# Graph layer on one core: an order of the loop in which the small products, the last odd message, the permutations and the class sums stand elsewhere

## The chip, the core and the metric

The kernel runs on one core of one Trainium2 chip. The metric is the device time of one execution in microseconds (us), lower is better. Five engines run queues of their own, each strictly in the order of its program, and meet through semaphores: TensorE (PE; its weight loads are a row of their own, PEld), VectorE (DVE), ScalarE (ACT), GpSimd (POOL, here the issuer of the indirect DMAs) and SyncE (SP, issuer of plain loads).

## The reference

A message passing layer over a graph with 6250 nodes and 206250 edges, features of 64, hidden width 128, all in float32:

```python
msg = jnp.concatenate([src_node_features[col], edge_attr], axis=1)
h = jax.nn.relu(msg @ W1a.T + b1a)
h = h @ W1b.T + b1b
sums = jax.ops.segment_sum(h, row, num_segments=n_nodes)
agg = sums / jnp.maximum(counts, 1.0)[:, None]
z = jax.nn.relu(jnp.concatenate([src_node_features, agg], axis=1) @ W2a.T + b2a) @ W2b.T + b2b
out = jnp.concatenate([z, src_node_features], axis=1) @ Wr.T + br
return layernorm(x + out)
```

`col` is the sorted end of each edge, `row` (the one summed over) is not sorted. The edges are therefore sorted by `row` on the chip while the messages are computed.

## The kernel before

**Tiles.** The edges are cut into 403 quads of 512 edges. A turn `m` of the main loop (202 of them, behind 22 turns of preparation) starts quads `2m` and `2m+1`. Nodes are 49 classes of 128. Every 31 quads are a block (13 in all), for which the places in the sorted store are worked out.

**What a quad goes through.** PE `hidden(q)` (L561) is the first layer: one float32 product of 512 columns into the bank HH. ACT `relu(q)` (L837) moves it to `hT`. PE `message(q, j)` (L570), j from 0 to 3, is the second layer: a float32 product of 64 columns with 128 weights of `hT` into the one bank MS, which holds the eight results of a pair of quads. ACT `copy_x` (L850) takes the whole bank MS as bfloat16, DVE `rest` (L1039) the remainder, ACT `middle_part` (L856) and DVE `low` (L1045) the second and third parts. So each float32 number is three bfloat16 numbers in Z. PE `permute(q, h)` (L591), h 0 and 1, is 6 products of 195 columns into PA or PBk with the 0/1 matrices M that DVE `places(q, h)` (L1054) makes; ACT `evict(q, h)` (L888) brings the bank to `stg`, and POOL scatters it to the sorted store `region` (L1348).

**Ranks.** PE `rank(i)` has four small products: L629 (counts of quad i+42, bank CK), L684 and L689 (ranks of quad i+5, 200 columns each, bank RK) and L700 (destination steps of quad i+4, 6 columns, bank RK). DVE `ranks(i)` answers with `positions(i+5)` (L1059), every fourth time with `destinations` (L1114, L1118), and once in a block each with `chain_counts`, `chain_places` and `chain_steps`. At its place in `rank(i)` PE waits for the positions before. Once in a block DVE also has `index` (L1003 to L1012). DVE further makes `classes` (L1021), `onehot` (L1031) and `stair` (L1105).

**Sums.** From turn 145 on, 46 turns (`sum_at`) also gather one class of the first segment back from `region`: ACT `ids` (L867), DVE `same_node` (L1179), 30 PE products of 195 columns in `class_sum` (L604, into columns 200 and up of bank RK), DVE `add_class`. Three further classes, all of the second segment and the node layers follow behind the loop. Those gathers may start only when the last scatter has landed.

**Order within a turn before.** PE: `hidden(2m)`, both halves of `permute(2m-3)`, `hidden(2m+1)`, `message(2m, 0)`, `rank(2m)` (in sum turns with `class_sum` behind L629), `permute(2m-2)` with the messages 1 to 3 of quad 2m among its products, `rank(2m+1)` with the messages 0 to 3 of quad 2m+1 among its products. From turn 142 (EARLY) on message 0 of the even quad stands inside the permutation. DVE: `ranks(2m-1)`, `rest` twice, the first `places` with `low` twice between, `classes`, `onehot`, `ranks(2m)`, `add_class`, `stair`, `places` of the next quad, `same_node` of the next sum. ACT: `relu`, `middle_part` twice, `evict` twice, `relu`, `ids`, `evict` twice, `copy_x`.

Waits that matter: `message(q, 0)` of an even quad waits until DVE has done both `rest` of the pair before (L567, `s_r`), for they read MS. `rest` waits for `copy_x` (`s_x`), `copy_x` for the last message of the odd quad (`s_msg`).

## Time and profile before

| | us |
|---|---|
| median of 3 runs | 1556.19 |
| lowest and highest | 1556.15, 1567.82 |
| span of the profiled execution | 1549.2 |
| PE busy | 1504.9 (97%) |
| DVE busy | 1403.3 (91%) |
| POOL busy | 1066.0 (69%) |
| ACT busy | 1040.7 (67%) |

The profiled execution's span, from its first to its last instruction, lies 7.0 us under the median of the runs. How to read: "busy" is the time in which an engine has at least one instruction under way. The chain that ended last is for 83% of the span on PE. TensorE's granted clock is 0.992 of full speed (2.4 GHz) over the span, and 1.00 in all of the main loop.

### The profile page before, as it was taken

The page shows a single profiled execution, that of the slowest core. Times are in us where ns is not written, and L with a number is a line of the kernel's source. Part 1 is how long each engine was busy: PE and PEld are TensorE (multiplying, and loading weights), DVE is VectorE, ACT ScalarE, POOL GpSimd, SP SyncE. Part 2 cuts the span into 40 slices and gives each one's busy share as a digit, 9 for nine tenths or more (in the row PEclk, how much of TensorE's full clock was granted, in tenths as well). Part 3 has the DMA queues.
Part 4 walks back from the last instruction along what each step waited for, and adds up shares of the span by engine and source line. Part 5 has one row for each costly group of instructions (what it writes and reads, how often), then busy time and mean ns, then how long its engine had stood idle before and what let it go on. Part 6 is the DMA issues. An engine that isn't in the chain of part 4 may idle for free.

```text
span 1549.2 us, 42475 instructions
## 1 busy us (share of the span) xinstructions
PE 1504.9 (97%) x13326; PEld 1246.8 (80%) x13326; DVE 1403.3 (91%) x4381; ACT 1040.7 (67%) x2211; POOL 1066.0 (69%) x929
## 2 busy tenths in 40 slices
PE   9999999999999999999999999999999999996897
PEld 6788888888888888888888888888888888876776
DVE  5899999999999999999999999999999999886886
ACT  2687878778777887878877775656555665672222
POOL 2467777677776777767777777778777777766541
PEclk9999999999999999999999999999999999998999
DMA  8566656566666665656656669999999999785997
GB/s 231 154 172 171 167 161 179 165 167 177 164 174 169 166 178 161 169 164 177 166 161 180 174 202 290 275 292 301 290 283 294 268 301 289 222 260 198 368 365 236
DMA packets 135506, 336.23 MB, mean 217 GB/s; under 512 B 36506, under 2 KB 69565, under 8 KB 129016
## 3 DMA queue, kind: packets, MB, share of 16 engines
q0 software_dynamic: 53184, 225.39, 45.2%
q1 hardware_dynamic: 81028, 104.05, 26.4%
q10 hardware_dynamic: 1076, 4.09, 1.0%
q8 instruction: 112, 1.84, 0.5%
q14 instruction: 106, 0.87, 0.2%
HBM read 213.48 MB, written 119.91 MB: 215 GB/s over the span
## 4 chain that ended last, share of the span: by engine, by line
PE 83%; DMA 5%; DVE 5%; issue 2%; POOL 2%; ACT 1%; POOLq 0%; DVEq 0%; ACTq 0%; SPq 0%
PE HH L561 22%; PE MS L570 19%; PE PA L591 12%; PE PBk L591 12%; PE RK L604 7%; DMA gbuf<-region,idx 4%; PE RK L684 2%; PE CK L629 2%; PE RK L689 2%; PE PA L604 1%; DVE OH L1179 1%; POOL region L1348 1%; DMA region<-stg,dest 1%; DVE M L1054 1%; POOL gbuf L1376 1%
## 5 line engine op out<-in xcount | busy, mean ns | idle before, releaser
L1348 POOL DMA_INDIRECT region<-stg,dest x806 | 932.0, 1156 | 380.1 <-issue 190.9
L570 PEld LDWEIGHTS MS<-W,hT 128*128 128x128 f32 x3224 | 478.8, 191 | 68.0 <-issue 62.7
L570 PE MATMUL MS<-W,hT 128*128 128x64 f32 x3224 | 509.4, 260 | 0.0
L561 PE MATMUL HH<-eab,pw 128*128 128x512 f32 x806 | 433.7, 620 | 1.9 <-ACT hT L837 1.9
L1054 DVE TENSOR_SCALAR M<-pos_of,pos 128x384 bf16<-128x384 int16 x1612 | 431.3, 318 | 0.2
L591 PE MATMUL PBk<-Z,M 128*128 128x195 bf16 x2418 | 338.7, 248 | 0.2 <-ACT stg L888 0.2
L591 PE MATMUL PA<-Z,M 128*128 128x195 bf16 x2418 | 315.2, 248 | 7.8 <-ACT stg L888 6.5
L888 ACT ACTIVATE stg<-PA 120x585 bf16<-120x585 f32 x403 | 263.5, 654 | 88.0 <-PE PA L591 82.2
L591 PEld LDWEIGHTS PA<-Z,M 128*128 128x128 bf16 x2418 | 214.0, 103 | 125.5 <-issue 119.9
L837 ACT ACTIVATE hT<-HH 128x512 f32<-128x512 f32 x403 | 241.9, 600 | 84.2 <-PE HH L561 84.2
L888 ACT ACTIVATE stg<-PBk 120x585 bf16<-120x585 f32 x403 | 265.3, 658 | 47.2 <-PE PBk L591 45.7
L591 PEld LDWEIGHTS PBk<-Z,M 128*128 128x128 bf16 x2418 | 233.8, 107 | 0.6 <-issue 0.4
L1059 DVE TENSOR_REDUCE pos<-RK 128x4 f32<-128x200 f32 x403 | 146.7, 364 | 49.0 <-PE RK L700 34.2
L856 ACT ACTIVATE Z<-Zr 128x256 bf16<-128x256 f32 x403 | 146.9, 413 | 52.7 <-DVE Zr L1039 52.4
L850 ACT ACTIVATE Z<-MS 128x512 bf16<-128x512 f32 x202 | 122.2, 605 | 85.4 <-PE MS L570 85.4
L1045 DVE TENSOR_TENSOR Z<-Zr,Z 128x256 bf16<-128x256 f32 x403 | 169.8, 421 | 4.6
L1179 DVE TENSOR_TENSOR OH<-laneb,ids 128x1920 bf16<-128x1920 bf16 (+2 forms) x110 | 161.8, 1487 | 12.5 <-ACT ids L867 12.4
L1039 DVE TENSOR_TENSOR Zr<-MS,Z 128x256 f32<-128x256 f32 x403 | 151.1, 415 | 16.4 <-ACT Z L850 16.2
L1031 DVE TENSOR_SCALAR eab<-kb,C 64x1024 f32<-64x1024 bf16 x202 | 153.1, 758 | 7.5 <-DMA kb<-keyd 1.0
L604 PEld LDWEIGHTS RK<-gbuf,OH 128*128 128x128 bf16 x1440 | 122.8, 97 | 22.4 <-issue 17.3
L604 PE MATMUL RK<-gbuf,OH 128*128 128x195 bf16 x1440 | 130.5, 247 | 3.1 <-DVE OH L1179 1.5
L561 PEld LDWEIGHTS HH<-eab,pw 128*128 128x128 f32 x806 | 122.0, 192 | 3.9 <-issue 3.7
(214 smaller groups left out, 1524.3 us busy)
## 6 DMA issues: line engine op xcount, KB each, us to landing
eab<-in_ea SPq DMA_DIRECT2D x201, 256.0 KB
kb<-keyd SPq DMA_DIRECT2D x201, 128.0 KB
pw<-ptab SPq DMA_DIRECT2D x403, 32.0 KB
region<-stg,dest POOLq DMA_INDIRECT x806
gbuf<-in_xt ACTq DMA_DIRECT2D x6, 422.5 KB
ptab<-OH SPq DMA_DIRECT2D x7, 256.0 KB, 3.2
gbuf<-region,idx POOLq DMA_INDIRECT x98, 8.9
eab<-in_xt SPq DMA_DIRECT2D x12, 130.0 KB
```

The costliest lines, as they stand in the source:

```text
L561: e.matmul(HH[:, :], pw[:, q % 4, :], eab[:, c % NB, at_q:at_q + GE], start=True, stop=True).then_inc(s_h, 1)
L570: ins = e.matmul(MS[:, o:o + D], hT[:, q % 2, 128 * j:128 * j + 128], W[:, W_1B:W_1B + D], start=True, stop=True)
L591: last = e.matmul(P[:, 256 * j:256 * j + 3 * PART].rearrange("p (k f) -> p k f", k=3), M[:, q % 2, 2 * h + t, j, :], Z[:, q // 2 % 2, 4 * ...
L604: last = e.matmul(o, onehots(s, c)[:, k, j, :], rows[:, ROW * k + LINE * j:ROW * k + LINE * j + 3 * PART], start=k == 0 and j == 0, stop=k ...
L837: e.activation(hT[:, q % 2, :], HH[:, :], ACT.Relu).then_inc(s_relu, 1)
L888: e.activation(stb[:, g % NS, :].rearrange("p (j f) -> p j f", j=R)[:, :, 0:3 * PART], P[0:KC, 0:768].rearrange("p (j f) -> p j f", j=R)[: ...
L1031: e.tensor_scalar(eab[64:128, c % NB, 0:w], kb[64:128, c % NB, 0:w], C[64:128, C_P64:C_P64 + 1], None, ALU.is_equal).then_inc(s_oh, 1)
L1039: e.tensor_tensor(Zr[:, j:j + 4, :], MS[:, j * D:j * D + 4 * D].rearrange("p (j f) -> p j f", f=D), Z[:, q // 2 % 2, j:j + 4, 0, 0:D], ALU ...
L1045: e.tensor_tensor(Z[:, q // 2 % 2, j:j + 4, 2, 0:D], Zr[:, j:j + 4, :], Z[:, q // 2 % 2, j:j + 4, 1, 0:D], ALU.subtract).then_inc(s_l, 1)
L1054: last = e.tensor_scalar(M[:, q % 2, t, :, :], pos_of[:, :, :], pos[:, q % 16, t:t + 1], None, ALU.is_equal)
L1179: last = e.tensor_tensor(onehots(s, c).rearrange("p k j (n u) -> p (k j) n u", u=2)[:, k:k + n, :, :], lane2[:, None, :, :].to_broadcast([ ...
L1348: e.indirect_dma_start(lines[s], bass.IndirectOffsetOnAxis(ap=dest[:, g:g + 1], axis=0), stw[:, g % NS, :], None).then_inc(s_sc[g % NS], 16)
```

## The change

- `rank`: L700 with its wait moves from behind L689 to ahead of L684. The wait for the positions is a function `bank_read` now. Message 3 of the odd quad leaves `rank` and is issued in the next turn, right behind `hidden` of the even quad.
- Permutations come half a turn later: `permute(2m-4)` behind that message, `permute(2m-3)` in the second half of the turn, with messages 1 to 3 of the even quad.
- `rank(2m)` stands before `hidden(2m+1)`, and `message(2m, 0)` always directly behind `hidden(2m+1)` (EARLY is gone). `class_sum` comes behind that message.
- A semaphore `s_even` tells `relu` of an even quad that its half of `hT` is free.
- ACT and DVE lists follow: `copy_x` comes behind the first `relu`; on DVE `same_node` (in a sum turn) or `places(2m-3)` and `classes` (in another) stand ahead of `rest`.

```diff
@@ schedule of the gathers
-        gather_at = {2 * (m - 3) - 2: c for m, c in sum_at.items()}
-        gather_at.update({2 * (max(sum_at) + k): NC - BEHIND + k for k in range(BEHIND)})
+        gather_at = {max(2 * (m - 3) - 3, BQ * SEGB[1] + NS // 2 - 1): c for m, c in sum_at.items()}
+        gather_at.update({2 * (max(sum_at) + k) - 1: NC - BEHIND + k for k in range(BEHIND)})
@@ PE, message
+                        if j == 3 and q % 2 == 0 and q < NQ - 1:
+                            ins.then_inc(s_even, 1)
@@ PE, rank
+                        bank_read(i)
...
-                        if i % 2 == 0 and i // 2 in sum_at:
-                            class_sum(sum_at[i // 2])
...
+                        q = i + 4
+                        if 0 <= q < NQ:
+                            b = q // BQ
+                            e.wait_ge(s_S, q // 2 + 1)
+                            k = 4 * (q % BQ)
+                            at_q = Q_DEST + 6 * (q % 4)
+                            last = e.matmul(RK[:, at_q:at_q + 6].rearrange("p (k g) -> p k g", g=2), S[:, q % 4, :],
+                                            Dzb[:, b % 2, :, k + 1:k + 4:2], start=True, stop=True)
                         q = i + 5
...
-                        if beside is not None:
-                            message(beside, 3)
-                        q = i + 4
-                        if 0 <= q < NQ:
...
@@ PE, a turn
                             hidden(2 * f)
-                        if 0 <= 2 * m - 3 < NQ:
-                            permute(2 * m - 3, 0)
-                            permute(2 * m - 3, 1)
+                        if m - 1 in front and 2 * front[m - 1] + 1 < NQ:
+                            message(2 * front[m - 1] + 1, 3)
+                        if 0 <= 2 * m - 4 < NQ:
+                            permute(2 * m - 4, 0)
+                            permute(2 * m - 4, 1)
+                        if m < 0:
+                            spin(e, HH, 4)
+                        rank(2 * m)
                         even = odd = None
...
                             hidden(odd)
-                        if even is not None and m < EARLY:
+                        if even is not None:
                             message(even, 0)
-                        if m < 0:
-                            spin(e, HH, 4)
-                        rank(2 * m)
-                        if 0 <= 2 * m - 2 < NQ:
-                            permute(2 * m - 2, 0, even)
-                            permute(2 * m - 2, 1, even)
+                        if m in sum_at:
+                            bank_read(2 * m + 1)
+                            class_sum(sum_at[m])
+                        if 0 <= 2 * m - 3 < NQ:
+                            permute(2 * m - 3, 0, even)
+                            permute(2 * m - 3, 1, even)
@@ ACT, relu
-                            e.wait_ge(s_msg, q // 2)
+                            e.wait_ge((s_even, s_msg)[q % 2], q // 2)
@@ ACT, a turn (the new order)
                             relu(2 * f)
                         if m - 1 in front:
+                            copy_x(front[m - 1])
+                        if 2 * m - 1 >= AMID[PB - 1]:
+                            copy_chain(2 * m - 1)
+                        if 0 <= 2 * m - 4 < NQ:
+                            evict(2 * m - 4, 0)
+                            evict(2 * m - 4, 1)
+                        copy_chain(2 * m)
+                        if f is not None and 2 * f + 1 < NQ:
+                            relu(2 * f + 1)
+                        if m - 1 in front:
                             for q in range(2 * front[m - 1], 2 * front[m - 1] + of_pair(front[m - 1])):
                                 middle_part(q)
...
+                        if next_sum(m) is not None:
+                            ids(0, next_sum(m))
                         if 0 <= 2 * m - 3 < NQ:
                             evict(2 * m - 3, 0)
                             evict(2 * m - 3, 1)
@@ DVE, a turn (the new order)
                         ranks(2 * m - 1)
+                        if m in sum_at:
+                            same_node(0, sum_at[m])
+                        elif 0 <= 2 * m - 3 < NQ:
+                            places(2 * m - 3, 0)
+                            places(2 * m - 3, 1)
+                        if 0 <= m + LEAD // 2 < NP and m not in sum_at:
+                            classes(m + LEAD // 2)
                         f = front.get(m - 1)
                         if f is not None:
                             for q in range(2 * f, 2 * f + of_pair(f)):
                                 rest(q)
...
+                        ranks(2 * m)
+                        if 0 <= m + LEAD // 2 < NP and m in sum_at:
                             classes(m + LEAD // 2)
                         if m + 1 in front:
                             onehot(front[m + 1])
-                        ranks(2 * m)
+                        if m in sum_at and 0 <= 2 * m - 3 < NQ:
+                            places(2 * m - 3, 0)
+                            places(2 * m - 3, 1)
+                        if f is not None:
+                            for q in range(2 * f, 2 * f + of_pair(f)):
+                                low(q)
                         if m in sum_at:
                             add_class(sum_at[m])
                         if 0 <= m + 3 < NP:
                             stair(m + 3)
-                        if 0 <= 2 * m - 1 < NQ:
-                            places(2 * m - 1, 0)
-                            places(2 * m - 1, 1)
+                        if 0 <= 2 * m - 2 < NQ:
+                            places(2 * m - 2, 0)
+                            places(2 * m - 2, 1)
```

## Rows read from the trace of the kernel before

**Rows 1.** The page: the span, and busy time (share of span) xinstructions.
```profile
span 1549.2 us, 42475 instructions
...
PE 1504.9 (97%) x13326; PEld 1246.8 (80%) x13326; DVE 1403.3 (91%) x4381; ACT 1040.7 (67%) x2211; POOL 1066.0 (69%) x929
```
**Rows 2.** Timeline of a plain turn: start us, us, engine line op tiles [idle before].
```profile
605.27 0.25 PE L689 MATMUL RK<-BS,sel 128*128 128x200 bf16 x1
...
605.36 0.36 PE L570 MATMUL MS<-W,hT 128*128 128x64 f32 x2
...
605.58 1.10 PE L561 MATMUL HH<-eab,pw 128*128 128x512 f32 x2
605.76 0.60 ACT L850 ACTIVATE Z<-MS 128x512 bf16<-128x512 f32 x1 [0.37 <-PE MS L570]
605.79 0.36 DVE L1059 TENSOR_REDUCE pos<-RK 128x4 f32<-128x200 f32 x1
...
606.07 0.17 DVE L1114 TENSOR_REDUCE dsum<-RK 120x8 f32<-120x24 f32 x1
...
606.42 0.75 DVE L1039 TENSOR_TENSOR Zr<-MS,Z 128x256 f32<-128x256 f32 x2
606.52 0.68 PE L591 MATMUL PA<-Z,M 128*128 128x195 bf16 x6
...
607.22 0.71 ACT L856 ACTIVATE Z<-Zr 128x256 bf16<-128x256 f32 x2
...
607.56 1.05 PE L561 MATMUL HH<-eab,pw 128*128 128x512 f32 x2
...
608.44 0.33 PE L570 MATMUL MS<-W,hT 128*128 128x64 f32 x2
...
608.47 0.42 DVE L1045 TENSOR_TENSOR Z<-Zr,Z 128x256 bf16<-128x256 f32 x1
...
608.61 0.25 PE L629 MATMUL CK<-OC,ind 128*128 128x200 bf16 x1
...
608.80 0.38 DVE L1021 TENSOR_TENSOR OC<-clsb,cls 128x400 bf16<-128x400 bf16 x1
...
608.89 0.51 PE L591 MATMUL PA<-Z,M 128*128 128x195 bf16 x4
...
610.39 0.31 DVE L1105 TENSOR_TENSOR S<-iotab,offs 128x240 bf16<-128x240 bf16 x1
...
610.50 0.36 PE L570 MATMUL MS<-W,hT 128*128 128x64 f32 x2
...
610.62 1.04 DVE L1054 TENSOR_SCALAR M<-pos_of,pos 128x384 bf16<-128x384 int16 x4
...
611.56 1.10 PE L561 MATMUL HH<-eab,pw 128*128 128x512 f32 x2
```
**Rows 3.** Timeline of a sum turn, the same columns.
```profile
1157.54 2.15 DVE L1179 TENSOR_TENSOR OH<-laneb,ids 128x3840 bf16<-128x3840 bf16 x1
...
1158.06 1.10 PE L561 MATMUL HH<-eab,pw 128*128 128x512 f32 x2
...
1159.61 0.36 DVE L1059 TENSOR_REDUCE pos<-RK 128x4 f32<-128x200 f32 x1
...
1166.62 1.10 PE L561 MATMUL HH<-eab,pw 128*128 128x512 f32 x2
```
**Rows 4.** Timeline of DVE where a block's work comes in, two stretches.
```profile
475.63 0.27 DVE L1003 TENSOR_TENSOR kd<-dc,baseB 128x124 int32<-128x124 int32 x1
...
476.62 0.35 DVE L1059 TENSOR_REDUCE pos<-RK 128x4 f32<-128x200 f32 x1
...
488.96 0.21 DVE L1072 CAST offs<-RK 128x62 bf16<-128x62 f32 x1
...
489.92 0.74 DVE L1039 TENSOR_TENSOR Zr<-MS,Z 128x256 f32<-128x256 f32 x2
```
**Rows 5.** Timeline of POOL at the end of the loop.
```profile
1401.10 0.99 POOL L1348 DMA_INDIRECT region<-stg,dest  x1 [0.30 <-issue]
```

More of the change, by code:

```diff
@@ L61 @@
 PIECES = 5
-EARLY = SUMS - 3
 SUMCOL = 200
@@ L596, in permute @@
                                     last.then_inc((s_pA, s_pB)[h], 1)
-                                if beside is not None and (h, j, t) in among(beside):
-                                    message(beside, among(beside)[h, j, t])
+                                if beside is not None and (h, j, t) in among:
+                                    message(beside, among[h, j, t])
                     def products(o, s, c):
@@ L612, in class_sum, with bank_read @@
                         products(sums(c), 0, c)
-                    def rank(i, beside=None):
-                        if not pe_ranks(i):
-                            for j in range(4 if beside is not None else 0):
-                                message(beside, j)
-                            return
-                        if beside is not None:
-                            message(beside, 0)
-                        last = None
-                        b = block_at(i - 1, 12)
-                        if b is not None:
-                            e.wait_ge(s_cc, COPIES * b + 2)
-                        q = i + 42
-                        if 0 <= q < NQ:
-                            e.wait_ge(s_oc, q // 2 + 1)
-                            k = q % BQ
-                            last = e.matmul(CK[:, 0:4 * CL], ind[:, 30 - k:158 - k],
-                                            OC[:, q % OCN, :, :].rearrange("p t c -> p (t c)"),
-                                            start=k == 0, stop=k == BQ - 1)
-                        if beside is not None:
-                            message(beside, 1)
+                    def bank_read(i):
                         if 0 <= i + 4 < NQ:
@@ L651, in rank @@
                             e.wait_ge(s_tab[1], 12)
+                    def rank(i, beside=None):
+                        if not pe_ranks(i):
+                            for j in range(3 if beside is not None else 0):
+                                message(beside, j)
+                            return
+                        if beside is not None:
+                            message(beside, 0)
+                        last = None
+                        b = block_at(i - 1, 12)
+                        if b is not None:
+                            e.wait_ge(s_cc, COPIES * b + 2)
+                        q = i + 42
+                        if 0 <= q < NQ:
+                            e.wait_ge(s_oc, q // 2 + 1)
+                            k = q % BQ
+                            last = e.matmul(CK[:, 0:4 * CL], ind[:, 30 - k:158 - k],
+                                            OC[:, q % OCN, :, :].rearrange("p t c -> p (t c)"),
+                                            start=k == 0, stop=k == BQ - 1)
+                        if beside is not None:
+                            message(beside, 1)
+                        bank_read(i)
                         if i % 2 and i // 2 in sum_at:
                             e.wait_ge(s_ad, 3 * sum_at[i // 2] + 3)
-                        if i % 2 == 0 and i // 2 in sum_at:
-                            class_sum(sum_at[i // 2])
                         b = block_at(i, 11)
@@ L910, in _ @@
                             evict(2 * m - 3, 1)
-                        if f is not None and 2 * f + 1 < NQ:
-                            relu(2 * f + 1)
-                        copy_chain(2 * m)
                         if f is not None:
                             copy_id(f)
-                        if next_sum(m) is not None:
-                            ids(0, next_sum(m))
-                        if 0 <= 2 * m - 2 < NQ:
-                            evict(2 * m - 2, 0)
-                            evict(2 * m - 2, 1)
-                        if f is not None:
-                            copy_x(f)
                     for c in range(NC - BEHIND + 2, NC):
@@ L1233, in _ @@
                                 rest(q)
-                        if 0 <= 2 * m - 2 < NQ:
-                            places(2 * m - 2, 0)
-                        if f is not None:
-                            low(2 * f)
-                        if 0 <= 2 * m - 2 < NQ:
-                            places(2 * m - 2, 1)
-                        if f is not None and of_pair(f) == 2:
-                            low(2 * f + 1)
-                        if 0 <= m + LEAD // 2 < NP:
+                        ranks(2 * m)
+                        if 0 <= m + LEAD // 2 < NP and m in sum_at:
                             classes(m + LEAD // 2)
@@ L1262, in _ @@
                                 totals(s)
-                        if next_sum(m) is not None and m < NP - 2:
-                            same_node(0, next_sum(m))
                     def add(p):
```

25 lines of the change are left out of this document (7 added, 18 removed).

## The prediction

> **What bounds the kernel now.** I read the page first: PE is busy 97% of the span, DVE 91% [rows 1]. Then the timeline of a plain turn. `hidden` of the even quad starts at 605.58 and that of the next pair at 611.56: 5.98 us a turn, in which PE's products follow each other without a hole [rows 2]. A sum turn lasts from 1158.06 to 1166.62, 8.56 us [rows 3], just as dense. So time can be won only by a shorter stream of PE, and lost by anything that makes PE wait. What the reader has to see next is how much room each wait has. Take the start of `hidden` of the even quad as 0. DVE begins `positions` at 0.21 (605.79) and ends both `rest` at 1.59 (606.42 and 0.75), while the next message into MS stands at 2.86 (608.44) [rows 2]. That is over a microsecond of room before PE would wait for `rest`.
>
> **PE's stream after the change.** Now message 3, L700 and `hidden` take 1.16 together (605.36 to 606.52) [rows 2]. Afterwards `hidden` follows a 200-column product, as the odd one now follows one of 195: 0.88 (607.56 to 608.44). Message 3 follows `hidden`, as message 0 does now: 0.17 (608.44 to 608.61). L700 stands between two bfloat16 products: four of them take 0.28 (608.61 to 608.89), three of 200 columns at 0.085 each, so 0.03 for it. The sum is 1.08, which saves 0.08 a turn [rows 2]. It is float32 weights that lie open behind a short product and are covered behind a long one. In a sum turn message 0 too goes from among the permutations (three of them with 12 products take 1.61, 608.89 to 610.50, so 0.19 each) to behind `hidden`, 0.17: 0.11 in all. Of 202 turns 46 are sum turns (49 classes less 3), which leaves about 155 steps: 155 x 0.083 = **-13 us**, and a sum turn of 8.45 us if nothing waits.
>
> The Trainium skill (TensorE: Matmul & The Clock Gate, "Step-by-step: what each phase is for") says that the next tile's weights load while the present product runs. Taken plainly, the order of products would then cost nothing and the -13 would be 0. The row speaks against it here: the same `hidden` takes 0.94 behind the 6 columns of L700 and 0.88 behind 195 [rows 2].
>
> **The new place of `rest`.** The new PE times of a turn, from the same rows: `hidden` to 0.88, message 3 to 1.05, 12 permutation products of 1.04 (606.52 to 607.56) to 2.09, `rank` 0.28 to 2.37, `hidden` to 3.25, and there stands `message(2m, 0)`, which waits for both `rest`. ACT needs `relu` first: `middle_part` starts 0.70 after the end of `hidden` now (606.52 to 607.22), and `copy_x` takes that place: it starts at 1.58, ends at 2.18 (0.60), and `rest` can start 0.05 later, at 2.21 to 2.24 (now 606.36 to 606.42) [rows 2]. From the end of `rest` to the message I take 0.05 for the signal and 0.09 to 0.11 for the weights, an estimate from 1246.8 us for 13326 loads [rows 1]. So `rest` must end by **3.10**, or PE stands still. Behind that message on PE are the sums, the permutation, the second `rank` and the next `hidden`, so every engine waits with it.
>
> *Plain turn.* `rest` at its earliest ends at 2.21 + 0.75 = 2.97. DVE's list before it: `positions` 0.28 (605.79 to 606.07), every other turn `destinations` 0.35 (606.07 to 606.42), four `places` 0.96 (1.04 less an overlap of 0.08), `classes` 0.38 [rows 2]. DVE's start x follows from the turn before. `low` waits for `middle_part`, which waits for the odd `hidden`: 3.25 + 0.70 + 0.41 = 4.36, `low` at 4.39; then two `low` of 0.33 (608.47 to 608.80), `stair` 0.23 (610.39 to 610.62), `places` 0.96: 6.24, less the turn of 5.90 gives x = 0.35 [rows 2]. So `rest` ends at 0.35 + 0.28 + 0.35 + 0.96 + 0.38 + 0.75 = 3.07 in the longer case: just in time. I take 0 for the stall; the seams between DVE's instructions that are new here have no row, and by the neighbouring ones are off by up to 0.1, in one turn of two. Kept for the range: 0 to +0.05 a turn, +8 us.
>
> *Sum turn.* Here x is 0.21, since DVE waits for the rank product. Ahead of `rest` stand `positions` 0.28 and `same_node`, 2.07 (1157.54 to 1159.61) [rows 3]. `rest` ends at 0.21 + 0.28 + 2.07 + 0.75 = 3.31, with `destinations` at 3.66. That is 0.21 and 0.56 past 3.10, 0.39 on the mean. `class_sum` then waits for the positions made after `rest`, about 0.05 more (estimate). PE's turn is 8.45 + 0.44 = 8.89 against 8.56 now: +0.33, times 46 = **+15 us**. With seams of 0.1 either way: +10 to +20. Now nothing of that shows, as `same_node` straddles the turn's start and message 0 stands behind the sum.
>
> *Blocks.* A block brings DVE extra work: `index` 0.99 (475.63 to 476.62) and `chain_places` 0.96 (488.96 to 489.92) [rows 4], and `chain_counts`, `chain_runs` and `chain_steps`, three or so small operations each, which I put at 0.5 to 0.8 by the same rows. Now a microsecond of room takes them in. Afterwards what comes ahead of `rest` finds 0 to 0.3 us of room (3.10 less 2.97 to 3.07, and DVE's pause for `copy_x`). `index` at a turn's end costs about 0.5 to 0.7 us in the next turn; what falls into `ranks` of an odd index costs 0.4 to 0.7, `chain_places` in every other block, counts and steps in the others. What falls behind `rest` is mostly taken in by the pause before `low` (about 0.3). I take 1.2 us a block less 0.3 for waits of `rank` on positions and chain that go away, since `rank(2m)` and `rank(2m+1)` now lie more evenly: 12 blocks x 0.9 = **+11 us**, bounds 0 and 20.
>
> *End of the loop.* The last scatters go out back to back, one in 1.30 (0.99 and 0.30 idle) [rows 5], and the second segment's gathers wait for them. With the permutations half a turn later POOL has one quad, two scatters, more to do: **+2.6 us**, bounds 0 and 3.
>
> The other moves cost nothing: both `relu`, `evict` and the two halves of a permutation keep half a microsecond or more between producer and consumer by the times above. The gathers are issued one quad earlier in number, which is the same moment.
>
> **Sum.** -13 + 15 + 11 + 2.6 = +16 us on the span of 1549.2 [rows 1], so 1565 there. The span lies 7.0 under the median, and the edits are within it: 1556.2 + 16 = **1572 us**, 1.0% slower.
>
> **Rivals.**
> - *The stream alone decides (other side).* If the Vector chain of a sum turn ends by 3.10, because `same_node` and its seams are shorter by 0.2 to 0.5, and blocks are taken in, then 1556.2 - 13 - 46 x 0.11 + 2.6 = 1541. For it: PE is the one full engine. Against it: 2.07 for `same_node` is a plain row.
> - *Sums wait, blocks don't.* 1572 - 11 = 1561. For it: DVE has pauses in each turn, and blocks are 3 of 15 turns.
> - *DVE bounds the plain turns too.* x creeps past 0.4 and every second message waits 0.1: 1572 + 8 = 1580.
> - *The new order saves nothing on PE.* Then 1572 + 13 + 5 = 1590. The page's rule above would have it so; the row is against it.
> - *Gain and loss cancel*: the waits cost half of what I take, 1556.
>
> **How the numbers follow.** Forecast 0.42, stream alone 0.08, sums only 0.25, DVE everywhere 0.15, cancel 0.07, no saving 0.03. The range of 1554 to 1588 leaves out the stream alone and no saving, and about 0.08 of the others' edges. A measurement of this kernel can tell about 1%, 15.6 us, from no change, so the borders are 1540.6 and 1571.8. The forecast lies on the upper one and goes two to one to "slower", the sums-only and cancel cases to "same": faster 0.06, same 0.45, slower 0.49.
>
> **What would show it.** Right: plain turns of 5.89 to 5.90 between the even `hidden`; in sum turns of about 8.7 and 9.05 by turns, a pause of TensorE in front of L570 ended by DVE Zr L1039; in blocks the same pause, up to 0.7. Wrong: sum turns of 8.45 (no stall), plain turns of 5.98 (no gain of the stream) or over 5.95 (DVE bounds), a last scatter that isn't later against the last `hidden`.

## The result and the profile after

On the chip of the result the changed kernel takes 1580.76 us (median of 4 runs, 1578.32 to 1582.63), the kernel before 1561.8 beside it (4 runs, 1556.15 to 1567.82): ratio on record 1.0142, 95% interval 1.0107 to 1.0177. So it is slower, by 1.4% by that ratio and by 1.2% (19.0 us) by the medians alone; the ratios on record, here and below, are not the quotients of the two medians, and lie up to 0.7 points off them. The profiled spans are 1577.3 and 1549.2 [rows 1], 28.1 apart, 9 more than the medians. About 5 of these come from the profiles: that of before lies 7.0 under the median of its first runs, that of after 1.9 under its own run (1579.23).

The page of the changed kernel: span, busy time (share) xinstructions, then the chain that ended last by engine, and one of its costliest groups (busy, mean ns | idle before, releaser).

```profile
span 1577.3 us, 42707 instructions
PE 1507.1 (96%) x13326; PEld 1249.6 (79%) x13326; DVE 1391.7 (88%) x4381; ACT 1018.8 (65%) x2211; POOL 1064.0 (67%) x929
...
PE 77%; DVE 10%; DMA 4%; issue 4%; ACT 2%; POOL 2%; DVEq 0%; POOLq 0%; ACTq 0%
...
L570 PEld LDWEIGHTS MS<-W,hT 128*128 128x128 f32 x3224 | 501.5, 191 | 241.0 <-DVE Zr L1042 132.8
```

No engine has a larger share of the span than before [rows 1]; DVE's share of the chain has gone from 5% to 10%. A group of the page of before was "PEld MS L570 <- DVE Zr L1039", 4.9 us in 17 waits. The same waits after (us in total, times, longest):

```profile
PEld MS L570 <- DVE Zr L1042: 132.8, 188, 2.3
PE MS L570 <- DVE Zr L1042: 23.2, 43, 1.5
```

(`rest` is L1042 now, `positions` L1062, the destination product L687, the ranks L692 and L697, `permute` L590, `class_sum` L603, `same_node` L1182, `copy_x` L853, `evict` L891, the scatter L1354.)

**A plain turn.** Timeline, start us, us, engine, line. Where a list ends with a first layer "x1", it shows the first of its two passes alone, and the turn ends at its start:

```profile
606.90 0.25 PE L697 MATMUL RK<-BS,sel 128*128 128x200 bf16 x1
606.99 1.05 PE L561 MATMUL HH<-eab,pw 128*128 128x512 f32 x2
607.43 0.35 DVE L1062 TENSOR_REDUCE pos<-RK 128x4 f32<-128x200 f32 x1
607.87 0.33 PE L570 MATMUL MS<-W,hT 128*128 128x64 f32 x2
...
608.56 0.60 ACT L853 ACTIVATE Z<-MS 128x512 bf16<-128x512 f32 x1
...
609.16 0.17 PE L687 MATMUL RK<-Dz,S 128*128 128x6 bf16 x1
609.18 0.25 PE L692 MATMUL RK<-OC,trib 128*128 128x200 bf16 x1
...
609.25 0.75 DVE L1042 TENSOR_TENSOR Zr<-MS,Z 128x256 f32<-128x256 f32 x2
...
610.24 0.33 PE L570 MATMUL MS<-W,hT 128*128 128x64 f32 x2
...
612.88 0.62 PE L561 MATMUL HH<-eab,pw 128*128 128x512 f32 x1
```

From 606.99 to 612.88: 5.89 us, against 5.98 [rows 2]. `positions` starts 0.44 into the turn, `rest` ends at 3.01, the message that needs it stands at 3.25.

**A sum turn** (1242.76 to 1251.42, 8.66 us, against 8.56 [rows 3]):

```profile
1242.76 1.05 PE L561 MATMUL HH<-eab,pw 128*128 128x512 f32 x2
...
1243.24 2.15 DVE L1182 TENSOR_TENSOR OH<-laneb,ids 128x3840 bf16<-128x3840 bf16 x1
...
1245.12 1.05 PE L561 MATMUL HH<-eab,pw 128*128 128x512 f32 x2
1245.31 0.75 DVE L1042 TENSOR_TENSOR Zr<-MS,Z 128x256 f32<-128x256 f32 x2
...
1246.11 0.30 PEld L570 LDWEIGHTS MS<-W,hT 128*128 128x128 f32 x2 [0.77 <-DVE Zr L1042]
...
1246.39 2.73 PE L603 MATMUL RK<-gbuf,OH 128*128 128x195 bf16 x30
...
1251.42 0.62 PE L561 MATMUL HH<-eab,pw 128*128 128x512 f32 x1
```

`rest` ends 3.30 into the turn and TensorE's weight load for the message waits for it. In the next sum turn `destinations` are in front too: `rest` ends at 3.67, and the turn takes 9.04.

**A block.** `index` at the end of DVE's list, and the two turns behind it (95.92 to 102.69, 102.69 to 110.12):

```profile
96.38 0.27 DVE L1006 TENSOR_TENSOR kd<-dc,baseB 128x124 int32<-128x124 int32 x1
...
97.49 0.36 DVE L1062 TENSOR_REDUCE pos<-RK 128x4 f32<-128x200 f32 x1
...
99.15 0.74 DVE L1042 TENSOR_TENSOR Zr<-MS,Z 128x256 f32<-128x256 f32 x2
...
99.95 0.43 PE L570 MATMUL MS<-W,hT 128*128 128x64 f32 x2 [0.61 <-DVE Zr L1042]
...
105.42 0.26 PE L648 MATMUL CK<-OC,ind 128*128 128x200 bf16 x1 [0.48 <-ACT BS L879]
```

`positions` starts 1.57 into the turn instead of 0.44, `rest` ends at 3.97. One turn later `rank` waits for a copy of the block's chain.

**The first sum turn**, around turn 145, which starts at 931.97:

```profile
926.18 1.06 POOL L1373 DMA_INDIRECT gbuf<-region,idx  x1 [0.30 <-issue]
...
931.97 1.05 PE L561 MATMUL HH<-eab,pw 128*128 128x512 f32 x2
...
936.74 0.26 ACT L870 ACTIVATE ids<-gbuf 128x60 bf16<-128x60 bf16 x1 [6.00 <-DMA gbuf<-region,idx]
937.69 0.69 PE L590 MATMUL PA<-Z,M 128*128 128x195 bf16 x6 [4.50 <-ACT stg L891]
```

The first gather is issued 5.79 us ahead of its turn. Before it was 9.29 ahead (920.65 against 929.94). From issue to the start of `ids` it takes 10.56 us (926.18 to 936.74), before 10.46 (920.65 to 931.11), so the late issue comes out in full: ACT waits 6.00 for it, before 3.11. `evict` stands behind `ids` on ACT, and PE waits 4.50 for `evict`, before 1.01. Behind that pause the clock adds to it: from 938.2 to 941.6 TensorE's granted clock is 0.50 of full speed, its lower level (1.2 GHz), where it was 1.00 ahead of the pause and is again behind 941.6. Half of these 3.4 us, 1.7, is lost work. The turn takes 14.76; 8.45 without a wait, 4.50 and 1.7 make 14.65. Before, the turn took 10.27 and the clock stayed at 1.00.

**The ledger.** The starts of the even first layers cut both profiled spans into turns; after less before, in us:

| stretch | forecast | measured |
|---|---|---|
| turns 3 to 144, stream alone (142 x -0.088) | -13 (155 turns) | -12.5 |
| the same turns, excess of the nine blocks (+14.1) and of turns 123 and 124 | +11 (12 blocks) | +14.8 |
| turn 145, the first sum turn | none | +4.5 |
| turns 146 to 192 (32 undisturbed sum turns among them, 8.84 against 8.53 on the mean, +10.0) | +15 (46 turns) | +16.4 |
| turns 193 to 200 | none | +1.2 |
| behind the last first layer | +2.6 | +4.0 |
| ahead of turn 3 | none | -0.3 |
| sum | +16 | +28.1 |

In the row of turns 193 to 200, turn 197 alone is 1.67 longer: a pause of 2.74 in front of a permutation, before 2.24, and behind it the granted clock at 0.50 from 1399.0 to 1405.8.

### The profile page after: what moved, and what is told of

Read it like the earlier page. It is cut to its first block, busy times and chain, and to the rows that moved or that the text cites. A ratio compares the mean times of both kernels' runs of the same rounds, so it can differ in the third digit from the quotient of the medians.

```text
span 1577.3 us, 42707 instructions
## 1 busy us (share of the span) xinstructions
PE 1507.1 (96%) x13326; PEld 1249.6 (79%) x13326; DVE 1391.7 (88%) x4381; ACT 1018.8 (65%) x2211; POOL 1064.0 (67%) x929
## 4 chain that ended last, share of the span: by engine, by line
PE 77%; DVE 10%; DMA 4%; issue 4%; ACT 2%; POOL 2%; DVEq 0%; POOLq 0%; ACTq 0%
PE MS L570 18%; PE HH L561 18%; PE PBk L590 11%; PE PA L590 11%; PE RK L603 7%; DMA gbuf<-region,idx 3%; PE RK L692 2%; DVE M L1057 2%; DVE Zr L1042 2%; PE CK L648 2%; PE PA L603 2%; PE RK L697 2%; DVE OH L1182 1%; DMA region<-stg,dest 1%; POOL region L1354 1%
## 5 line engine op out<-in xcount | busy, mean ns | idle before, releaser
L1354 POOL DMA_INDIRECT region<-stg,dest x806 | 920.8, 1142 | 408.9 <-ACT stg L891 228.0
L570 PEld LDWEIGHTS MS<-W,hT 128*128 128x128 f32 x3224 | 501.5, 191 | 241.0 <-DVE Zr L1042 132.8
L570 PE MATMUL MS<-W,hT 128*128 128x64 f32 x3224 | 530.4, 260 | 23.6 <-DVE Zr L1042 23.2
L561 PE MATMUL HH<-eab,pw 128*128 128x512 f32 x806 | 424.1, 608 | 1.3 <-ACT hT L840 0.8
L840 ACT ACTIVATE hT<-HH 128x512 f32<-128x512 f32 x403 | 240.6, 597 | 261.0 <-PE HH L561 259.5
L891 ACT ACTIVATE stg<-PA 120x585 bf16<-120x585 f32 x403 | 265.6, 659 | 117.7 <-PE PA L590 114.2
L590 PE MATMUL PBk<-Z,M 128*128 128x195 bf16 x2418 | 339.2, 249 | 0.2 <-DVE M L1057 0.2
L590 PE MATMUL PA<-Z,M 128*128 128x195 bf16 x2418 | 306.1, 249 | 8.0 <-ACT stg L891 7.5
L891 ACT ACTIVATE stg<-PBk 120x585 bf16<-120x585 f32 x403 | 270.3, 671 | 20.4 <-PE PBk L590 17.2
L590 PEld LDWEIGHTS PA<-Z,M 128*128 128x128 bf16 x2418 | 228.9, 111 | 8.8 <-issue 7.9
L590 PEld LDWEIGHTS PBk<-Z,M 128*128 128x128 bf16 x2418 | 235.0, 108 | 0.8 <-DVE M L1057 0.4
L1048 DVE TENSOR_TENSOR Z<-Zr,Z 128x256 bf16<-128x256 f32 x403 | 153.6, 424 | 46.5 <-ACT Z L859 44.9
L1062 DVE TENSOR_REDUCE pos<-RK 128x4 f32<-128x200 f32 x403 | 143.3, 356 | 43.8 <-PE RK L697 40.8
L1182 DVE TENSOR_TENSOR OH<-laneb,ids 128x1920 bf16<-128x1920 bf16 (+2 forms) x110 | 161.7, 1486 | 17.4 <-ACT ids L870 17.1
L1042 DVE TENSOR_TENSOR Zr<-MS,Z 128x256 f32<-128x256 f32 x403 | 150.9, 415 | 13.2 <-ACT Z L853 11.7
L859 ACT ACTIVATE Z<-Zr 128x256 bf16<-128x256 f32 x403 | 144.6, 410 | 1.3 <-DVE Zr L1042 1.2
L603 PE MATMUL RK<-gbuf,OH 128*128 128x195 bf16 x1440 | 130.9, 247 | 2.4 <-DVE OH L1182 1.7
L561 PEld LDWEIGHTS HH<-eab,pw 128*128 128x128 f32 x806 | 121.7, 191 | 2.2 <-issue 1.9
L603 PEld LDWEIGHTS RK<-gbuf,OH 128*128 128x128 bf16 x1440 | 120.3, 97 | 2.8 <-issue 2.8
L853 ACT ACTIVATE Z<-MS 128x512 bf16<-128x512 f32 x202 | 121.3, 600 | 0.0
```

Source lines behind the costliest of these rows:

```text
L561: e.matmul(HH[:, :], pw[:, q % 4, :], eab[:, c % NB, at_q:at_q + GE], start=True, stop=True).then_inc(s_h, 1)
L570: ins = e.matmul(MS[:, o:o + D], hT[:, q % 2, 128 * j:128 * j + 128], W[:, W_1B:W_1B + D], start=True, stop=True)
L590: last = e.matmul(P[:, 256 * j:256 * j + 3 * PART].rearrange("p (k f) -> p k f", k=3), M[:, q % 2, 2 * h + t, j, :], Z[:, q // 2 % 2, 4 * ...
L603: last = e.matmul(o, onehots(s, c)[:, k, j, :], rows[:, ROW * k + LINE * j:ROW * k + LINE * j + 3 * PART], start=k == 0 and j == 0, stop=k ...
L840: e.activation(hT[:, q % 2, :], HH[:, :], ACT.Relu).then_inc(s_relu, 1)
L891: e.activation(stb[:, g % NS, :].rearrange("p (j f) -> p j f", j=R)[:, :, 0:3 * PART], P[0:KC, 0:768].rearrange("p (j f) -> p j f", j=R)[: ...
```

## The experiments

The runs of this section come from three different chips; whether the chip of the result is one of them isn't known. On them the kernel before took 1860.44, 1832.42 and 1862.82 us, 17 to 19% more than beside the result. So times are compared on one chip only, and mechanisms by turns that came through undisturbed. On none of the three was a profile of the kernel before taken; where turns are compared with it, the kernel before with L700 moved stands in for it.

**First chip: the destination product alone, in the kernel before.**

```diff
@@ rank, of the kernel before
+                        (L700 and its wait, ahead of L684)
                         q = i + 5
...
-                        (L700 and its wait, behind L689 and message 3)
```

> The kernel before, with one part of the change alone: L700 (destination product) and its wait stand ahead of L684 in rank. Nothing else moves. If the order of PE's stream is what gains (0.94 against 0.88 for a first layer behind 6 columns or behind 195): a plain turn of 5.92 instead of 5.98 and a sum turn of 8.50 instead of 8.56, no new wait, about 12 us faster than the kernel before, 1544 to 1549. If weight loads are hidden whatever the order: plain turns stay at 5.98 and the time stays at that of the kernel before.

Measured: 1867.02 (1850.92 to 1887.78, 10 runs) against 1860.44 (13 runs), ratio 1.0043 (0.9996 to 1.0091). The time is the same within the noise. Undisturbed turns took 5.946 (12 of them), against 5.977 on the chip of the result. The same kernel on the second chip:

> The kernel before with L700 ahead of L684 alone. In the first trace of it the undisturbed turns took 5.95 (not 5.92: I had left out that L700 costs 0.03 at its new place too). So 0.03 a turn, 6 us, faster than the kernel before where the stream of PE bounds (0.996), and no difference where DMAs bound.

Measured: 1836.66 against 1832.42, ratio 1.0015 (0.9981 to 1.0049); undisturbed turns again 5.946. So in the order of before the place of L700 is worth 0.03 us a turn, half of what I expected (the 0.03 that L700 takes at its new place I had left out), and no time that can be measured. In that order a first layer behind a message starts the next product 0.91 after itself (764.30 to 765.21, rows below), between the 0.94 behind L700 and the 0.88 behind 195 columns [rows 2].

**First chip: message 0 behind the class sum in sum turns, in the changed kernel.**

```diff
+                    def among(q):
+                        if q // 2 in sum_at:
+                            return {(0, 0, 1): 0, (0, 2, 0): 1, (1, 0, 1): 2, (1, 2, 0): 3}
+                        return {(0, 1, 1): 1, (1, 0, 1): 2, (1, 2, 0): 3}
...
-                        if even is not None:
+                        if even is not None and m not in sum_at:
                             message(even, 0)
```

> The changed kernel, but in sum turns message 0 of the even quad goes back among the permutation's products, behind the class sum. If two waits stand behind each other at that place (message 0 for rest, then the class sum for the positions that DVE makes after rest), taking the first away moves the stall to L603 and sum turns stay at about 8.65 and 9.0. If rest alone was the cause, sum turns fall to about 8.47 and the run is about 18 us faster than the changed kernel.

Measured: 1820.11 (one run). Undisturbed sum turns are not shorter: 8.86 and 8.81 where the changed kernel has 8.67 and 8.61. TensorE's pause now stands in front of `class_sum`: it starts 1.26 and 1.35 behind the odd first layer, where 0.88 would do, so the pause is 0.4 to 0.5 us, and 0.85 in the sum turns with `destinations` (9.19). In the undisturbed turns without `destinations` `class_sum` starts at 3.63 in both kernels. Two waits stood one behind the other: `class_sum` needs `positions`, which DVE makes behind `rest`. Taking the first away lays the second bare.

**Both waits taken away:** message 0 as above, and in sum turns DVE's `ranks(2m)` ahead of `rest`.

```diff
                         f = front.get(m - 1)
+                        if m in sum_at:
+                            ranks(2 * m)
                         if f is not None:
                             for q in range(2 * f, 2 * f + of_pair(f)):
                                 rest(q)
-                        ranks(2 * m)
+                        if m not in sum_at:
+                            ranks(2 * m)
```

> As the run before it, and in sum turns DVE answers rank(2m) (positions) ahead of both rest. Both waits are then off the path: sum turns of 8.45 to 8.50, 0.4 less than in the changed kernel, 46 of them, so 16 to 19 us faster than the changed kernel: 1562 to 1565. If something else holds the sum turns (gathers, the one-hots of same_node), they stay above 8.6.

Timeline of an undisturbed sum turn of this kernel (1532.25 to 1540.57; `class_sum` is L606 here, `rest` L1045, `same_node` L1185):

```profile
1532.25 1.05 PE L561 MATMUL HH<-eab,pw 128*128 128x512 f32 x2
...
1532.73 2.15 DVE L1185 TENSOR_TENSOR OH<-laneb,ids 128x3840 bf16<-128x3840 bf16 x1
...
1534.80 0.36 DVE L1065 TENSOR_REDUCE pos<-RK 128x4 f32<-128x200 f32 x1
1535.07 0.75 DVE L1045 TENSOR_TENSOR Zr<-MS,Z 128x256 f32<-128x256 f32 x2
1535.41 2.72 PE L606 MATMUL RK<-gbuf,OH 128*128 128x195 bf16 x30
...
1540.57 0.62 PE L561 MATMUL HH<-eab,pw 128*128 128x512 f32 x1
```

The sum starts 0.88 behind the odd first layer (1534.53) without a pause; the turn takes 8.33, where the changed kernel has 8.61 with the same work, and the other kind of turn 8.47 against 8.67. So in sum turns without `destinations` the stall is gone, and that shows its cause. With `destinations` ahead of both, a part of it stays: the least disturbed turns of that kind (168, 184 and 192) take 8.75, 8.72 and 8.49, where the changed kernel has 9.02, 8.96 and 8.96, and `class_sum` starts at 3.51, 3.54 and 3.32 instead of 3.25, 3.16 and 3.16. Against the one-wait kernel turns 146 to 192 are 13.9 us shorter in sum. Time: 1807.92 (1801.81 to 1814.26, 4 runs), ratio to before 0.9716 (0.9648 to 0.9784).

**The first sum turn: sums one turn later.**

```diff
-SUMS = 145
+SUMS = 146
```

> The changed kernel with all class sums one turn later (SUMS 146 instead of 145). Theory: the 14.8 us turn in which the sums begin comes from ScalarE, which waits for the first gather ahead of the evictions; the gather is issued half a turn later than before, as it hangs on a scatter of a permutation. One more turn of distance takes most of the 4.5 us of PE's pause away: 3 to 5 us faster than the changed kernel, the first sum turn below 11. Rival: the first gather takes as long as the DMA queues need to drain whenever it is issued; then the pause stays at 4 to 5 us.

Measured: 1813.99 (one run). Turns 144 to 146 take 9.11, 7.74 and 11.10, in sum 27.95; in the kernel with message 0 moved, on the same chip, they take 11.16, 10.14 and 9.24, 30.54. The 2.6 less is what a plain turn in place of a sum turn gives anyway, and that sum has to be done later; the first sum turn, 11.10, is not below the 11 that I expected either. But the run can't test the theory, for what was to be removed isn't there on this chip: in neither of the two kernels does ACT pause in front of the first `ids` (it starts 12.7 and 8.9 us behind the gather's issue; the result has a pause of 6.00 there). The gather did get more distance: it follows quad 283 instead of 282 (`gather_at`), while its sum went back by two quads. That a late gather is the cause of the long turn is therefore read from the rows of the result, where gather, `ids`, `evict` and permutation follow each other; it is not shown by an experiment.

**Second chip: the changed kernel.**

> The changed kernel once more, as the control for the others of this call. In the call before, the kernel before took 1860 us where the shown runs took 1556, with waits for landing DMAs throughout, so a chip is to be compared with itself alone. If the chip is as in the shown runs: 1.4% slower than the kernel before, plain turns 5.89, sum turns 8.67 and 9.04. If it is as in the call before: the order with the permutations half a turn later gives evictions and scatters more distance and the changed kernel is 2 to 3% faster than the kernel before, as the other variants of it were.

Measured: 1771.76 (1766.4 to 1780.99, 4 runs) against 1832.42 (13 runs): ratio 0.9635 (0.9588 to 0.9681). Here the changed kernel is *faster*, by 3.7% by that ratio and by 3.3% by the medians. By turns, against the kernel before with L700 moved: turns 3 to 144 -72.8 us, sum turns +10.3, behind the loop +9.2. The changed kernel loses in sum turns and at the end here too, but not in turn 145 (10.23 against 10.14); the gain ahead of it is another than in the result. The waits of both (us in total, times, longest), first the kernel before with L700 moved:

```profile
DVE pos L1059 <- remote: 184.7, 67, 4.3
...
ACT Z L850 <- remote: 100.2, 51, 3.0
PE HH L561 <- ACT hT L837: 98.5, 70, 2.6
```

and the changed kernel on the same chip:

```profile
PEld MS L570 <- DVE Zr L1042: 179.2, 165, 2.4
...
DVE pos L1062 <- remote: 104.5, 59, 5.6
...
ACT Z L853 <- remote: 5.9, 6, 1.1
...
PE HH L561 <- ACT hT L840: 2.4, 4, 1.2
```

"remote" is a releaser that the profile can't name. In the profiles of the chip of the result it does not occur among the larger waits, for either kernel. What it looks like (the kernel before with L700 moved, second chip):

```profile
764.02 0.25 PE L697 MATMUL RK<-BS,sel 128*128 128x200 bf16 x1
764.10 0.36 PE L570 MATMUL MS<-W,hT 128*128 128x64 f32 x2
764.30 1.08 PE L561 MATMUL HH<-eab,pw 128*128 128x512 f32 x2
765.21 0.68 PE L591 MATMUL PA<-Z,M 128*128 128x195 bf16 x6
...
767.64 0.37 DVE L1059 TENSOR_REDUCE pos<-RK 128x4 f32<-128x200 f32 x1 [4.12 <-remote]
767.68 0.60 ACT L850 ACTIVATE Z<-MS 128x512 bf16<-128x512 f32 x1 [2.92 <-remote]
...
768.18 0.59 ACT L837 ACTIVATE hT<-HH 128x512 f32<-128x512 f32 x1
...
768.91 1.47 PE L561 MATMUL HH<-eab,pw 128*128 128x512 f32 x2 [2.51 <-ACT hT L837]
```

L697 is over at 764.27 by its row, and `positions`, which reads its result, starts at 767.64; TensorE's semaphore events of all these products stand between 767.6 and 767.85 in the records. In the order of before, by the rows, ACT meets such a late signal in `copy_x` (L850), `relu` (L837) of the even quad stands behind it on ACT, and the odd first layer waits for `relu`: TensorE's gaps between a permutation and that first layer come to 120 us in turns 3 to 144 (84 gaps), those in front of the permutations behind `rank` to 48 (54). In the changed order `relu` of the even quad stands ahead of `copy_x`, and a whole permutation lies between message 3 and its reader. Both kinds of gap are gone (the wait of L561 for L840 is 2.4 us in the whole kernel); the largest kind now is the one between a first layer and the message behind it, 62 us (110 gaps). That the new lists of ACT and PE are the cause is read from the waits; no run changes them alone.

The 72.8 us of turns 3 to 144 split into TensorE's idle time, 160.0 against 111.3 (49 less), and its busy time, 943.25 against 919.08 (24 less). Of the 24 the stream gives 8 (142 x 0.057). The other 16 fit the granted clock, which differs a good deal: in these turns it is at the lower level for 109 us in the order of before (26 stretches) and for 31 us in the changed one (7 stretches), 0.95 and 0.99 on the mean, with 1.00 for both kernels beside the result. So part of the gain is most likely a clock that falls less often; it can't be split from the waits here, since the falls may themselves come of the pauses.

> The changed kernel with message 0 behind the class sum and the positions ahead of rest in sum turns. Expected from the undisturbed sum turns of its first trace: 8.47 where DVE has no destinations to make and 8.74 where it has, mean 8.60, against 8.67 and 9.04, mean 8.86. 46 turns: 10 to 13 us faster than the changed kernel, about the time of the kernel before plus 10 on a chip as in the shown runs.

Measured: 1763.6 (1752.85 to 1787.42, 4 runs), ratio to before 0.9558 (0.9505 to 0.961). Turns 146 to 192 are 13.1 us shorter than in the changed kernel on the same chip, at the upper end of what I expected. The median is 8 us lower, and the ranges of the runs overlap; without the one run of 1787.42 the other three have a median of 1758.77, 13 lower.

> As the run before it, and with two more moves: the sums begin one turn later (SUMS 146), and DVE's index of a block stands behind onehot, in DVE's pause ahead of low, instead of at the turn's end. Theory of the blocks: index at the turn's end pushes rest past 3.10 and costs 0.87 or 1.16 a block (turns of 6.77 and 7.05 instead of 5.89); in the pause it costs 0.3 or less: 12 blocks, 7 to 10 us. First sum turn: 3 to 5 us. Together 10 to 15 us faster than the run before it, which on a chip as in the shown runs is at the time of the kernel before or a few us under it. Rival: index delays low, stair and places of its turn by the same amount and PE then waits for those.

Its edit beside the two above is SUMS 146 and `index` moved up:

```diff
                         if m + 1 in front:
                             onehot(front[m + 1])
+                        for i in (2 * m + LEAD + 2, 2 * m + LEAD + 3):
+                            if i % BQ == 0 and 0 < i < NQ:
+                                index(i // BQ)
```

Measured: 1758.75 (1744.13 to 1770.47, 4 runs), ratio 0.9548 (0.9469 to 0.9628), the lowest median on this chip. I had expected 10 to 15 us less than the run before it; it is 4.9, with ranges that overlap, so a gain of the two added moves is not shown.

**Third chip.** The changed kernel as the base:

> The changed kernel once more, beside the kernel before on whatever chip this lands on, as the base for the next three. Theory 1 (the verdict belongs to the chip: where the kernel before takes about 1556 us the change costs some 1.4%, where it takes 1830 us or more the change gains some 3.5%): 1.010 to 1.018 in the first case, 0.96 to 0.97 in the second. Theory 2 (the 0.9635 was of one chip alone and the slow chips differ among each other): a ratio between 0.98 and 1.00 on a slow chip.

Measured: 1809.16 (1794.97 to 1814.92, 4 runs) against 1862.82 (7 runs), ratio 0.9697 (0.9627 to 0.9766). Theory 1 holds as far as it was tried: where the kernel before takes 1556 us the change loses, and where it takes 1830 or more it gains 3 to 4%, twice. Whether it is the chip or the hour that makes the difference, these runs don't tell apart.

> The changed kernel with message 0 behind the class sum and ranks(2m) ahead of rest in sum turns, index behind onehot instead of at the turn's end, and SUMS 146. If the waits of the first layer's neighbours on rest are what the changed kernel loses: sum turns of 8.33 and 8.47 undisturbed (46 x 0.33 = 15 us less), turn 145 of 7.7 and a first sum turn of 11.1, index turns 0.5 to 0.8 shorter than in the changed kernel; 18 to 25 us less than the changed kernel in the same call, and faster than the kernel before on a fast chip too (about 1558 against 1562, ratio 0.995 to 1.000; on a slow chip 0.95 to 0.96). If the waits only move (rival): within 5 us of the changed kernel.

Measured: 1792.94 (1789.38 to 1797.53, 4 runs), ratio 0.962 (0.9566 to 0.9673), 16 us below the changed kernel, where I expected 18 to 25. Turns 146 to 192 are 7.8 shorter than there, turns 3 to 144 6.3 longer, which is noise of that chip as far as I can tell. So this version is ahead of both kernels on two chips; under the conditions of the result it wasn't tried.

> The changed kernel with index moved from the turn's end to behind onehot, in the same turn, all else as it is. If index costs what was forecast (0.5 to 0.7 in the next turn, for rest comes later by it): turns behind an index lose their pause in front of the message, in all 12 times 0.5 to 0.9, 6 to 10 us. If the pause in those turns comes from something else of the block (chain_runs at the same place): the same turns stay as long as in the changed kernel.

Measured: 1809.89 (one run), no gain. The nine stretches of three turns around an `index` (up to turn 144) have medians of 23.2 us, and 22.9 in the changed kernel on the same chip. But this chip can't show what was asked. In its plain turns far from a block `positions` starts 1.82 into the turn in the median, in the changed kernel 1.75, where the result has 0.45; in the turn behind an `index` it starts between 0.24 and 3.60, in the changed kernel between 0.25 and 1.98. The 1.1 us by which an `index` delays it in the result is lost in that. So the expected gain of 6 to 10 us did not show in one run, and whether the place of `index` in DVE's list matters stays open. In the profile of the result DVE pauses in a plain turn 0.36 ahead of `low` (605.48, ended by ACT L859) and, in turns without `destinations`, 0.44 ahead of `rest` (603.31, ended by ACT L853), so there is little room for 1.0 us of extra work at either place.

> The changed kernel with the destination product back behind the two rank products, where the kernel before has it (6 columns directly ahead of message 0 to 2 or of the next first layer). If a first layer behind 6 columns lies open by its weights and behind 200 columns doesn't: undisturbed plain turns of 5.95 to 5.97 instead of 5.89, and the first layer of the even quad 0.06 longer. If the place is free (rival): 5.89 to 5.90.

```profile
481.81 0.17 PE L698 MATMUL RK<-Dz,S 128*128 128x6 bf16 x1
481.84 1.10 PE L561 MATMUL HH<-eab,pw 128*128 128x512 f32 x2
482.78 0.33 PE L570 MATMUL MS<-W,hT 128*128 128x64 f32 x2
```

Measured: 1803.41 (one run; the total says nothing on 10 us here). The six undisturbed plain turns take 6.015 in the median, against 5.889: +0.126, twice what I expected. The first layer behind the 6 columns takes 0.94 (481.84 to 482.78), behind 200 columns 0.88 (606.99 to 607.87), and this happens twice a turn, since `rank(2m)` now stands ahead of the odd first layer too. This shows the stream's gain to be the place of the destination product: without it, the new order would have been slower than before in plain turns as well (6.015 against 5.977). Within the first layer the rows put the 0.06 between its two passes: the second starts 0.51 behind the first when 6 columns stand ahead (605.58 to 606.10 before), 0.45 when 195 do (607.56 to 608.01), with weight loads of 0.19 in both. That fits weights that lie open, but what the run shows is the place alone.

## Why the prediction was right, and where it was off

- *Plain turns.* Forecast 5.89 to 5.90, measured 5.89. The removal shows that the gain is the product ahead of the first layer; that it is the weights which lie open behind 6 columns fits the rows. The reading of "message 3, L700 and `hidden`" as one sum of 1.16 hid that the move pays twice in the new order and that the rest of the order costs 0.04.
- *Sum turns.* Forecast 8.7 and 9.05 by turns, measured 8.67 and 9.04; `rest` ends at 3.30 and 3.67, forecast 3.31 and 3.66. The cause is shown by its removal, for the turns without `destinations`. The prediction had `class_sum` wait for `positions` too, at 0.05 behind the first wait; with message 0 out of the way the same wait is 0.4 to 0.9, so the two are nearly one, and only both moves together free the sum turns. Over 32 undisturbed sum turns the loss is 0.31 a turn, forecast 0.33.
- *DVE's start in a plain turn* was 0.44 instead of 0.35, and `rest` still ended in time (3.01), because `copy_x`, not DVE, is last in every second turn. The rival in which DVE bounds plain turns did not come.
- *Blocks.* The total of +11 stood for 12 blocks at 0.9. Measured as excess over plain turns, a block costs 2.09 us before and 3.66 after (nine blocks up to turn 144), +1.57. So nine blocks alone cost 14.1 where 12 were to cost 11. The term was mis-sized: the delay by `index` is 1.1 in `positions` and 0.9 to 1.2 in the turn (forecast 0.5 to 0.7), and the 0.3 that I took off, for fewer waits of `rank` on the chain, was of the wrong sign: that turn has 1.54 over a plain one now (0.48 of it a pause of `rank` for a copy of the chain), 0.92 before.
- *The first sum turn* was missing from the sum: +4.5. I had written that the gathers are issued at the same moment. For the first one this fails: the `max` in `gather_at` keeps it behind quad 282, as before, while the others go one quad earlier, and that quad's permutation comes half a turn later. Its lead is 5.79 us instead of 9.29. I had no term for the clock either, which gives 1.7 of the turn's cost.
- *End of the loop.* The last scatter is issued 18.85 us behind the start of the last first layer, 16.40 before: +2.45, forecast 2.6. A further 1.5 comes behind it, and the clock is of that size: from 1463.9 to 1467.3 it is granted at 0.50, which the kernel before does not have there, and the chain that ended last runs through it. The view of that chain (start us, us, what), first before, then after:

```profile
1445.22 1.44 PE PA L604 x15
1446.66 0.45 PE PBk L776 x4
```

```profile
1464.04 2.61 PE PA L603 x15
1466.65 0.81 PE PBk L779 x4
```

- *The sum* was thus 12 us short on the spans (28.1 against 16): 4.5 for the first sum turn, 3.8 for the blocks, 1.4 for turns 146 to 192, 1.4 at the end and 1.2 in turns 193 to 200. All of these miss in the same direction. The median of 1580.76 is 8.8 above the forecast, inside the range. That the medians differ by 19.0, so near to the 16, is luck: 9 us of what the profiles show between the two kernels is not in the runs.
- *The rival "no saving on PE"* falls: the undone step costs 0.126 us a turn, which is 142 x 0.126 = 18 us up to turn 144. The Trainium skill (TensorE: Matmul & The Clock Gate, "Step-by-step: what each phase is for") says that the next tile's weights load while the present product runs. The rows agree that the two overlap (the load of a first layer starts with L700's product, at 605.56), but to conclude that the order of products is free is wrong here, by the 0.126.

Open: what makes TensorE's signals late in the experiments and not beside the result, what a block costs by the place of its work, and what the versions without the double wait would do under the conditions of the result. For the last of these an estimate from rows: steady sum turns of 8.60 instead of 8.85 on the mean (8.47 and about 8.73 for 8.67 and 9.03), 46 times, give back some 12 us, and turns 146 to 192 were 13.1 and 13.9 shorter on the other chips. That is about two thirds of the 19 us lost, an estimate and not a run.

## What to carry to other kernels

Where a float32 first layer must follow small products, put the narrowest of them ahead of the wide ones and not directly in front; here each such place cost 0.06 us. When a wait is found behind a wait on the same two engines, take both away in one experiment; either alone can show nothing or a loss. When work is moved half a turn later, go through the one-time events too (first gather, last scatter, block work), for a steady turn shows none of them. And look at the granted clock behind each long pause: here it cost 1.7 us on top of one of 4.5.

## What was unexpected of the hardware

The same program took 1556 to 1568 us beside the result and 1824 to 1875 on three other occasions, on three chips, and the change was worth +1.4% in the first case and -3.7% and -3.0% on two of the three. The granted clock is part of it: 0.992 in the profile of the kernel before, 0.951 to 0.967 in its runs on the three chips (the changed kernel 0.988, and 0.974 and 0.971 in its profiles on two of them). In the profile with L700 moved on the second chip it is at the lower level for 151 us in 35 stretches, beside the result for 27 in 3, so at most some 62 of the 281 us between these two spans can be lost to it. The larger difference in the trace is idle time: readers of TensorE's signals start up to 3.4 us after the products have ended. The Trainium skill (Perfetto Trace Analysis, "Tensor Engine Instruction (MATMUL, LD_WEIGHTS)") says that the end of a product in the profile is estimated from its size, and that its semaphore goes out only when PSUM has acknowledged the write. So the rows don't tell a late signal from a product that really ended late, and no run here tells them apart either. The changed order, with more distance between producer and reader, lost less by it here: 111 us of idle time on TensorE in turns 3 to 144, against 160. The verdict of one chip at one time on a change of the order should be read with that in mind.
